# Experts stage: the owners of 18 tiles in one register load instead of 6, and a semaphore for each of four early sums

## The reference

```
rh = jax.nn.relu(features @ router_w1 + router_b1)
expert_logits = jax.nn.softmax(rh @ router_w2 + router_b2, axis=-1)
top_w, top_i = jax.lax.top_k(expert_logits, TOP_K)
routing_weights = jax.nn.softmax(top_w, axis=-1)
h1 = jax.nn.relu(jnp.einsum('bsd,edh->bseh', features, expert_w1) + expert_b1)
h2 = jax.nn.relu(jnp.einsum('bseh,ehf->bsef', h1, expert_w2) + expert_b2)
expert_out = jnp.einsum('bsef,efo->bseo', h2, expert_w3) + expert_b3
sel = jnp.take_along_axis(expert_out, top_i[:, :, :, None], axis=2)
combined = jnp.sum(sel * routing_weights[..., None], axis=2)
```

## Time and profile before

| | us |
|---|---|
| median of 3 runs | 3046.49 (3036.64 to 3049.08) |
| the profiled execution, its own time | 3039.37 |
| span of the profiled execution | 3037.6 |
| PE busy in the span | 2343.2 (77%) |
| DVE, POOL, ACT busy | 2164.0, 1995.0, 1172.0 |

### The profile page before, as it was taken

One profiled execution on the slowest core, in us unless ns is written; L12 is line 12 of the kernel. 1 busy time (PEld: TensorE's weight loads), 2 busy tenths in 40 slices (PEclk: granted clock), 3 DMA queues, 4 the chain that ended last, 5 costly groups with the idle time before them and its releaser, 6 DMA issues. The chain is left out here.

```text
span 3037.6 us, 76113 instructions
## 1 busy us (share of the span) xinstructions
PE 2343.2 (77%) x15555; PEld 1937.5 (64%) x15556; DVE 2164.0 (71%) x6024; ACT 1172.0 (39%) x4767; POOL 1995.0 (66%) x2241
## 2 busy tenths in 40 slices
PE   6587878888888887847777777777777757499897
PEld 4466667676666666636666666666666536378786
DVE  7477878787877786647777778777787655666565
ACT  3244545444444444513333333333333442322222
POOL 4577777777777774577777777777777225166665
PEclk9799989999999999859988989898888857699999
DMA  9755655565555553256566556655555248444432
GB/s 255 207 169 156 172 157 166 166 171 160 166 168 168 157 167 86 86 146 180 159 178 175 168 169 175 176 167 173 172 169 167 62 140 271 121 160 152 122 116 86
DMA packets 295113, 484.48 MB, mean 159 GB/s; under 512 B 69669, under 2 KB 204989, under 8 KB 295045
## 3 DMA queue, kind: packets, MB, share of 16 engines
q0 software_dynamic: 96384, 286.92, 33.3%
q1 hardware_dynamic: 134340, 150.23, 17.1%
q10 hardware_dynamic: 64320, 46.56, 4.9%
HBM read 404.17 MB, written 81.43 MB: 160 GB/s over the span
## 5 line engine op out<-in xcount | busy, mean ns | idle before, releaser
L703 POOL DMA_INDIRECT e_rows<-table,e_idx x1664 | 1580.2, 950 | 557.1 <-issue 403.4
L1087 PE MATMUL e_ps_sum<-e_hot,e_msg 128*128 128x129 f32 x6656 | 1118.6, 306 | 267.3 <-DVE e_msg L744 210.6
L1087 PEld LDWEIGHTS e_ps_sum<-e_hot,e_msg 128*128 128x128 f32 x6656 | 920.9, 205 | 427.0 <-ACT parts L942 242.2
L941 ACT ACTIVATE acc<-e_ps_sum 128x256 f32 x1664 | 639.0, 384 | 1222.8 <-PE e_ps_sum L1087 1022.7
L744 DVE TENSOR_TENSOR e_msg<-e_rows,e_ps_pr 128x256 f32<-128x256 f32 x1664 | 654.6, 415 | 82.0 <-issue 12.9
L723 DVE TENSOR_TENSOR e_hot<-e_ps_pr,rel 128x512 f32<-128x512 f32 x416 | 285.4, 686 | 163.2 <-PE e_ps_sum L1087 157.7
L1069 PE MATMUL e_ps_al<-e_dst_score,e_hotT 128*128 x3328 | 301.6, 180 | 1.5 <-issue 0.7
L1069 PEld LDWEIGHTS e_ps_al<-e_dst_score,e_hotT 128*128 128x128 bf16 x3328 | 251.5, 99 | 60.1 <-issue 2.3
L942 ACT ACTIVATE parts<-e_ps_sum 128x4 f32 (+1 forms) x1664 | 280.4, 168 | 0.0
L1076 PE MATMUL e_ps_al<-ident,e_lr 128*128 128x128 f32 x104 | 38.6, 371 | 171.8 <-DVE e_lr L768 170.8
L2010 ACT ACTIVATE x_h<-x,eb 128x128 f32<-128x128 f32 x216 | 67.4, 363 | 260.8 <-PE x L2079 260.8
(11 more groups left out here) (319 smaller groups left out, 3400.4 us busy)
## 6 DMA issues: line engine op xcount, KB each, us to landing
e_relb<-rel_rows SPq DMA_DIRECT2D x104, 512.0 KB
e_rows<-table,e_idx POOLq DMA_INDIRECT x1664
e_eattr<-in_edge_b SPq DMA_DIRECT2D x104, 128.0 KB
e_xT<-turned_x ACTq DMA_DIRECT2D x100, 128.0 KB
e_xr<-in_x ACTq DMA_DIRECT2D x100, 128.0 KB
node<-acc SPq DMA_DIRECT2D x25, 512.0 KB, 3.8
table<-t_row SPq DMA_DIRECT2D x25, 276.0 KB, 4.1
table<-j_row SPq DMA_DIRECT2D x25, 276.0 KB, 2.5
```

What stands on the lines that cost most here:

```text
L703: nc.gpsimd.indirect_dma_start(out=rows[q][:, k, :], out_offset=None, in_=table, in_offset=bass.IndirectOffsetOnAxis(ap=idx[:, q, k:k + 1] ...
L941: nc.scalar.activation(acc[:, :, bass.ds(at[k], P)], ps_sum[(k + q) % 3][:, :, 0:P], ACT.Copy).then_inc(s["window"], 1)
L1087: op = nc.tensor.matmul(ps_sum[(k + q) % 3][:, a, 0:WIN], msg[:, k % RM, a * P:a * P + P], hot[:, q, k, :], start=(a == 0), stop=True, ski ...
```

## The change

RUN = 18 takes the place of 6 as the size of a group: 108 tiles are 6 groups instead of 18, ACT and PE load 18 registers, DVE 20, and each looped body holds 18 tiles. The buffers of `y` stay six. Besides, the four gathers into `z` signal four semaphores, z0 to z3, and DVE waits before each of the four sums for its own.

```diff
--- before.py
+++ after.py
@@ -1910,6 +1910,7 @@
     ew, eb, eb3 = v["ew"], v["eb"], v["eb3b"]
     RY = 6
     AHEAD = 4
+    RUN = 3 * RY
     with ExitStack() as ctx:
         def tmp(name, shape, dt=F32):
             return sb("x_" + name, shape, dt, ctx)
@@ -1925,7 +1926,8 @@
         ps_1 = [pb(f"x_1{q}", [P, 512], ctx) for q in range(2)]
         ps_2 = [pb(f"x_2{q}", [P, 512], ctx) for q in range(2)]
         ps_3 = [pb(f"x_3{q}", [P, 512], ctx) for q in range(2)]
-        names = ("y0", "y1", "y2", "y3", "y4", "y5", "put0", "put1", "put2", "put3", "put4", "put5", "z", "pad",
+        names = ("y0", "y1", "y2", "y3", "y4", "y5", "put0", "put1", "put2", "put3", "put4", "put5",
+                 "z0", "z1", "z2", "z3", "pad",
                  "yt", "ytc", "h1", "h1c", "h2", "h2c", "o", "oc", "w", "on")
         s = {n: sem("x_" + n, ctx) for n in names}
         block = ctx.enter_context(nc.Block())
@@ -1955,7 +1957,7 @@
 
                 nc.gpsimd.indirect_dma_start(
                     out=z[:, t - TH, :], out_offset=None, in_=mid,
-                    in_offset=bass.IndirectOffsetOnAxis(ap=who[:, t:t + 1], axis=0)).then_inc(s["z"], 16)
+                    in_offset=bass.IndirectOffsetOnAxis(ap=who[:, t:t + 1], axis=0)).then_inc(s[f"z{t - TH}"], 16)
 
             def store(t):
 
@@ -1989,13 +1991,13 @@
 
         @block.scalar
         def _(act):
-            regs = [act.alloc_register(f"x_act{k}") for k in range(RY)]
+            regs = [act.alloc_register(f"x_act{k}") for k in range(RUN)]
             act.sem_inc(s["ytc"], 2)
             act.sem_inc(s["h1c"], 2)
-            with act.Fori(0, TT // RY) as i:
-                act.reg_load(regs, owner[0:1, bass.ds(RY * i, RY)])
-                for k in range(RY):
-                    t, q = RY * i + k, k % 2
+            with act.Fori(0, TT // RUN) as i:
+                act.reg_load(regs, owner[0:1, bass.ds(RUN * i, RUN)])
+                for k in range(RUN):
+                    t, q = RUN * i + k, k % 2
                     e = act.snap(regs[k], min_val=0, max_val=NEXP - 1)
                     act.wait_ge(s["yt"], t + 1)
 
@@ -2013,22 +2015,22 @@
 
         @block.vector
         def _(vec):
-            regs = [vec.alloc_register(f"x_vec{k}") for k in range(RY + 2)]
+            regs = [vec.alloc_register(f"x_vec{k}") for k in range(RUN + 2)]
 
             def weights(k, e):
 
                 nc.vector.tensor_copy(w[:, k % 2].rearrange("p m a f -> p m (a f)"),
                                       ew[:, 0:2, bass.ds(e, 1)].rearrange("p m e a f -> p m (e a f)")).then_inc(s["w"], 1)
 
-            def six(i, j, first=False, later=False):
-                vec.reg_load(regs, owner[0:1, bass.ds(RY * i, RY + 2)])
-                own = [vec.snap(regs[k], min_val=0, max_val=NEXP - 1) for k in range(RY + 2)]
+            def run(i, j, first=False, later=False):
+                vec.reg_load(regs, owner[0:1, bass.ds(RUN * i, RUN + 2)])
+                own = [vec.snap(regs[k], min_val=0, max_val=NEXP - 1) for k in range(RUN + 2)]
                 if first:
                     vec.wait_ge(s["on"], 1)
                     weights(0, own[0])
                     weights(1, own[1])
-                for k in range(RY):
-                    t, q = RY * i + k, k % 2
+                for k in range(RUN):
+                    t, q, u = RUN * i + k, k % 2, k % RY
                     e = own[k]
                     vec.wait_ge(s["h2"], t + 3)
 
@@ -2045,30 +2047,30 @@
                     vec.wait_ge(s["on"], 1)
                     nc.vector.tensor_tensor(raw[:], ps_3[q][:, 0:F], eb3[:, bass.ds(e, 1), :].rearrange("p e f -> p (e f)"), ALU.add)
                     vec.drain()
-                    so_far = y[:, k, 0:F]
+                    so_far = y[:, u, 0:F]
                     if later and k < AHEAD:
-                        vec.wait_ge(s["z"], 16 * AHEAD)
+                        vec.wait_ge(s[f"z{k}"], 16)
                         so_far = z[:, k, 0:F]
-                    nc.vector.scalar_tensor_tensor(y[:, k, 0:F], raw[:], y[:, k, 2 * F + j:2 * F + j + 1], so_far,
+                    nc.vector.scalar_tensor_tensor(y[:, u, 0:F], raw[:], y[:, u, 2 * F + j:2 * F + j + 1], so_far,
                                                    ALU.mult, ALU.add).then_inc(s["oc"], 1)
 
             vec.sem_inc(s["h2c"], 2)
             vec.sem_inc(s["oc"], 2)
-            six(0, 0, first=True)
-            with vec.Fori(1, TH // RY) as i:
-                six(i, 0)
-            six(TH // RY, 1, later=True)
-            with vec.Fori(TH // RY + 1, TT // RY) as i:
-                six(i, 1)
+            run(0, 0, first=True)
+            with vec.Fori(1, TH // RUN) as i:
+                run(i, 0)
+            run(TH // RUN, 1, later=True)
+            with vec.Fori(TH // RUN + 1, TT // RUN) as i:
+                run(i, 1)
 
         @block.tensor
         def _(pe):
-            regs = [pe.alloc_register(f"x_pe{k}") for k in range(RY)]
+            regs = [pe.alloc_register(f"x_pe{k}") for k in range(RUN)]
 
             def turn(k, i):
 
-                pe.wait_ge(s[f"y{k % RY}"], 16 * (i + k // RY) + 16)
-                pe.wait_ge(s["ytc"], RY * i + k + 1)
+                pe.wait_ge(s[f"y{k % RY}"], 16 * (RUN // RY * i + k // RY) + 16)
+                pe.wait_ge(s["ytc"], RUN * i + k + 1)
                 for a in range(2):
                     op = nc.tensor.transpose(ps_y[k % 2][:, a * P:a * P + P], y[:, k % RY, F + a * P:F + a * P + P], ident[:])
                 op.then_inc(s["yt"], 1)
@@ -2101,20 +2103,20 @@
                                           ew[:, 2, bass.ds(e, 1), h, :].rearrange("p e f -> p (e f)"), start=(h == 0), stop=(h == 1))
                 op.then_inc(s["o"], 1)
 
-            def six(i, begin=False, end=False):
-
-                pe.reg_load(regs, owner[0:1, bass.ds(RY * i, RY)])
-                e = [pe.snap(regs[k], min_val=0, max_val=NEXP - 1) for k in range(RY)]
+            def run(i, begin=False, end=False):
+
+                pe.reg_load(regs, owner[0:1, bass.ds(RUN * i, RUN)])
+                e = [pe.snap(regs[k], min_val=0, max_val=NEXP - 1) for k in range(RUN)]
                 if begin:
                     turn(0, 0)
                     turn(1, 0)
                     first(0, 0)
-                for k in range(RY):
-                    t = RY * i + k
+                for k in range(RUN):
+                    t = RUN * i + k
                     second(t, k)
-                    if not end or k < RY - 2:
+                    if not end or k < RUN - 2:
                         turn(k + 2, i)
-                    if not end or k < RY - 1:
+                    if not end or k < RUN - 1:
                         first(t + 1, k + 1)
                     third(t, k, e[k])
 
@@ -2122,10 +2124,10 @@
             pe.sem_inc(s["h1"], 2)
             pe.sem_inc(s["h2"], 2)
             pe.sem_inc(s["o"], 1)
-            six(0, begin=True)
-            with pe.Fori(1, TT // RY - 1) as i:
-                six(i)
-            six(TT // RY - 1, end=True)
+            run(0, begin=True)
+            with pe.Fori(1, TT // RUN - 1) as i:
+                run(i)
+            run(TT // RUN - 1, end=True)
 
 
 INS = ["x", "src_t", "dst_t", "dst_g", "first_row", "last_row", "fix_t", "edge_b", "W1", "W2", "att", "we", "cols", "Wqkv",
```

## The result

| us | before | after |
|---|---|---|
| median of 20 runs each | 3046.52 (3036.64 to 3050.84) | 3051.72 (3047.38 to 3057.53) |
| ratio, 95% interval | | 1.0021 [1.0012, 1.0029] |
| the profiled execution, its own time | 3039.37 | 3052.84 |
| experts stage: first load of owner to the end of the span | 401.8 | 409.2 |

The kernel became slower by 0.2%, 5.2 us, where a gain of 5 was forecast. Twenty runs of each kernel tell this from no change; it is well under the 0.5% that the prediction named. The stage shows it too. Before, its first load starts at 2635.8 in a span of 3037.6. After, it starts at 2641.9. The parts ahead of the stage thus differ by 6 us in two executions of the same code, which is why I compare the stage and not the span.

A forecast was written before the change was run, and what follows sets the result against it. PE was taken as the last stage's bound (busy 344 of 390 us), its idle time winnable. Loads 6.4 plus sums 3.4 gave 9.8 us less, 2.2 with the low clock each time; 5 was chosen: 3039, range 3024 to 3052.

The forecast's parts named there:

- the rival of PE's code: Looped body of 18 tiles doesn't fit, fetches at three back edges: about 3047; chance 0.07 of over 0.5% slower, 0.15 showing.
- the low clock: After idle of about 4 us PE runs slow: 2.9 us a dear boundary, 1.8 in the middle, 7.6 in all.
- The loads: Register loads at boundaries, by alignment: dear ACT 4.8, DVE 4.7, PE 5.6 us; cheap ACT 1.5, DVE 1.4.
- Long loads are cheap: Rival for boundary loads: each further register costs 0.03 us, gain 21.9 + 3.4 = 25 us; chance 0.12.
- I choose 5, nearer the second: Final choice of a 5 us gain, between 9.8 without the low clock and 2.2 with it each time.
- never a low clock: Case where PE's clock never falls at the boundaries: they cost 28.4 us, and the whole gain is 9.8.
- each time: Case where PE's clock falls at each dear boundary and the middle: boundaries cost 36.0 us, whole gain 2.2.
- Boundary costs of before: Group boundaries of the kernel before: eight dear at 3.1 us, eight cheap at 1.15, middle 0.8; sum 34.8.
- the middle's 0.8: Ninth boundary of the kernel before: dear, but only ACT's 0.8 us counts, the rest covered by a longer wait.
- A beat longer by 0.04 over 90 tiles is 3.6 us; same side: Rival that POOL's store and fetch become the bound, with fewer stalls to catch up: 3.6 us; no chance given.
- So 3.4 us are won, and PE's slow third and second layers are inside that wait: Mid-stage, tile 54's sum goes earlier with its own semaphore, then tile 58's rows are late: 3.4 us won, bounds 0 to 6.6.

The follow-up runs named there:

- e3: The kernel before with owner laid out 8 numbers to a group of six, so every load starts at a multiple of 16 bytes; ratio to before 0.9960.
- e4: The changed kernel with owner laid out 20 numbers to a group of 18, all loads from multiples of 16 bytes; ratio to before 0.9963.
- a0: The changed kernel itself, measured once more in another session; 3053.78 us, ratio to before 1.0012.
- e9: The changed kernel, unaligned loads kept, with nine buffers of y and rows fetched five tiles ahead; 3051.50 us, ratio to before 1.0004.
- e5: e4 with nine buffers of y instead of six and rows fetched five tiles ahead instead of four; 3021.67 us, ratio to before 0.9928.
- e2: The kernel before, groups of six kept, with only the four semaphores for z added; ratio to before 0.9987.

## Why the prediction was wrong

A gain of 5 us was forecast and a loss of 5.2 came. That the time lay in the range was luck: its upper end, 3052, was set by the rival of PE's code, which is false, and the measured 3051.72 lies 0.3 us inside. Two steps failed: late rows stood in the sum at nothing, and the low clock at 4.8 of the 7.6 us that the working gave for it. Step by step:

**The loads: right, but for PE's.** The dear ones of ACT, DVE and PE are 4.1 to 4.6, 4.5 to 4.9 and 4.3 us against 4.8, 4.7 and 5.6, the cheap ones of DVE and ACT 1.4 and 1.7 against 1.4 and 1.5. They alternate as foreseen, and e3 and e4 show that the address decides. The rival *Long loads are cheap* is false.

**PE's code: the rival is false.** The instruction queues have 33 and 48 packets against 26 and 43, 12 more for the whole program, which would be enough for three back edges. Where they fall decides. From 2770 to 2980, where PE goes back three times (its loads there start at 2780.5, 2842.0 and 2911.4), the view of the DMA queues has no packet of q8, and of q14:

```profile
q14 instruction: 5, 0.04, 0.1%
```

None of these five is within 10 us of a back edge. The Trainium skill ("Runtime: NRT & Kernel Launch", Instruction fetch mechanics) says that a taken branch whose target is out of the two-page window forces a fetch; this body of 792 products and weight loads shows none, and whether a larger one would, no run here shows.

**"I choose 5, nearer the second": this step failed.** The forecast lay between never a low clock and a low clock each time. It came each time. The first idle time at the first boundary was 3.75 us, near the 4 foreseen; the second was 1.90 and not 4, since the layers ahead of it ran slow, and the clock was still low behind it. For the four boundaries the working gave 24.4 us without the clock and 30.2 with it; measured are 29.7 and, in a0, 27.4. The case "each time" was right almost in full, and the 2.8 us that I added to its gain were not there. The profile before had told this already: one idle time of 3.83 us, and a slow row behind it.

**Boundary costs of before: mis-sized.** 34.0 us without the middle's 0.8 were worked out, and 31.3 are measured by the starts of the third layers. The tile behind a boundary takes 2.96 us and not 3.08, which I left out, and most dear boundaries cost less than 3.1. So there was less to win by 2.7.

**"A beat longer by 0.04 over 90 tiles is 3.6 us; same side": this step failed, and it is the largest.** That rows might come late stood among the rivals and not in the sum. Inside the groups tiles cost 1.2 us before and 7.2 after (5.2 in a0), and e9 and e5 take the cost away by a longer lead alone. The mechanism is near the one named there, but not the same. The beat isn't longer: from third layer to third layer the median is 3.087 us before and 3.084 after, and POOL's stores don't fall behind. What is gone is the time in hand. Before, three tiles behind most stalls have rows that landed about 1 to 3 us ahead of their turn, and the three after them mostly under 0.3; then the next stall comes. In groups of 18 it doesn't come. Of the 7.2 us, 3.0 are four gathers of 4.00 to 4.42 us that PE waited for, and 3.6 are in 33 tiles whose turn starts as their rows land, each a little late. So taking the stalls away couldn't win their whole length.

**"So 3.4 us are won, and PE's slow third and second layers are inside that wait": half right.** The next thing late was tile 58's rows, as foreseen. But the wait for them (4.04 us in e2) brought the low clock again, and 1.9 us were won alone, 2.5 with the large groups. In the changed kernel the sum of tile 54 had no wait left, since DVE's load of 4.9 us and the slow third layer held it longer. Of the middle in all, 14.2 us were to be expected (12.6 less ACT's 0.8, plus its 4.0, less 3.4, plus 1.8 for the clock); measured are 15.0.

**The sum, put right.** With the low clock each time the forecast was 2.2 us less. Add 6.0 for late rows, 2.7 for before's boundaries and 0.8 for the middle, and take away 0.5 for after's boundaries: 6.8 us more, the difference of the two traces (51.8 - 45.0). The terms are read from the same two traces, so that they add up says only that none was forgotten. a0's trace has 3.2 more (48.2 - 45.0), the timed runs 5.2 and 2.9.

## What to carry to other kernels

Before fewer and larger loads are tried, look at why half of the loads are dear: the address was worth 11 us of stage here (e3), the size of the group and the semaphores perhaps 3 more once the loads were aligned (e4; no more than two traces of one kernel differ). A short stall that comes often may be what gives a partner its time in hand (here the fetches with a lead of four tiles); before it is merged into a few long ones, read how much time lies between the landing of the rows and their use where nothing stalls, and hold the slowest transfers against it. And a stall that grows from under 2 us to about 4 us also costs the slow matmuls behind it: take those at their full price where the trace of before has one such place.

## What was not expected of the hardware

A register load's time hangs on the start address: 8 registers take 0.60 us from a multiple of 16 bytes and 1.85 from other multiples of 8; 20 take 1.36 and 4.5 to 4.9, by the same instruction on the same engine (e3 and e4 against before and after). The low clock of PE after a long stall doesn't always end at the same place: behind the dear boundaries the same tile cost 2.6 us more in e9 and between -0.1 and 2.0 in the two traces of the changed kernel.
